# A fused MoE / matrix-LSTM / MoE block on one core: heads normalised without the division, first state copied, squares and sums on ScalarE

## The reference

```python
def step(carry, inp):                       # 8 heads of 64, one token after the other
    c, n, m = carry
    qt, kt, vt, it, ft = inp
    m_t = jnp.maximum(ft + m, it)
    ie = jnp.exp(it - m_t)
    fe = jnp.exp(ft - m_t + m)
    c = fe[:, :, None, None] * c + ie[:, :, None, None] * jnp.einsum('bhd,bhe->bhde', vt, kt)
    n = fe[:, :, None] * n + ie[:, :, None] * kt
    num = jnp.einsum('bhde,bhe->bhd', c, qt)
    den = jnp.maximum(jnp.sum(n * qt, -1, keepdims=True), 1.0)
    return ((c, n, m_t), num / den)
...
h = o * jnp.moveaxis(hs, 0, 1).reshape(Bs, Sl, HID)
hn = _layernorm(h.reshape(Bs, Sl, H, HD), mh_g, mh_b).reshape(Bs, Sl, HID)   # per head, eps 1e-6
out = (hn + x_skip) * jax.nn.silu(r_t)
return out @ W_down.T + b_down + x
```

## Time and profile before

| what | value |
|---|---|
| median of 3 runs | 446.38 us (444.79 to 449.3) |
| the profiled run | 445.47 us |
| its span, first to last instruction | 443.2 us |
| TensorE busy | 384.7 us, 87% |
| VectorE busy | 340.3 us, 77% |
| ScalarE busy | 225.1 us, 51% |
| GpSimd busy | 126.4 us, 29% |
| the three looped sequences and the last | about 127 to 376 us of the span |

### The profile page before, as it was taken

How to read it: one execution, slowest core, us unless ns; L and a number is a source line. 1 busy time by engine, 2 the same in 40 slices (tenths; PEclk the granted TensorE clock), 3 DMA queues, 4 the chain that set the end, 5 groups by cost and what they waited for, 6 DMA issues and landing times.

```text
span 443.2 us, 11327 instructions
## 1 busy us (share of the span) xinstructions
PE 384.7 (87%) x3607; PEld 300.6 (68%) x3629; DVE 340.3 (77%) x1057; ACT 225.1 (51%) x591; POOL 126.4 (29%) x125
## 2 busy tenths in 40 slices
PE   8159999999998899998899898899889957699991
PEld 5023899954776667776668676678667744499991
DVE  4881677767729998969989779999699998567871
ACT  3630444434465565555674555485555651475550
POOL 5574154432003011103110121111021128644552
PEclk9555999999999999999999999999998998989998
DMA  7995122239998787775000000000000522333320
GB/s 208 377 414 187 29 70 71 59 108 214 185 185 185 176 184 177 181 178 124 1 0 0 0 0 0 0 0 0 1 1 1 200 76 83 115 102 93 92 79 1
DMA packets 57264, 46.10 MB, mean 104 GB/s; under 512 B 4111, under 2 KB 53905, under 8 KB 56721
## 3 DMA queue, kind: packets, MB, share of 16 engines
q1 hardware_dynamic: 53618, 37.84, 35.4%
q0 software_dynamic: 2752, 5.73, 3.7%
q10 hardware_dynamic: 864, 2.15, 1.5%
HBM read 17.99 MB, written 27.25 MB: 102 GB/s over the span
## 4 chain that ended last, share of the span: by engine, by line
issue 40%; PE 24%; DVE 11%; POOL 9%; DMA 6%; ACT 4%; SPq 2%; DVEq 1%; POOLq 0%; ACTq 0%
PE bank L896 22%; POOL HS L567 5%; POOL slots L519 3%; DMA K<-consts 2%; DMA XN<-slots 2%; DMA X<-x 1%; ACT WVT L786 1%; PE bank L1033 1%; ACT E L795 1%; POOL LA L561 1%; SPq L418 1%; ACT SELQ L674 1%; DMA QKT<-by_token 1%; DVE W1R L2009 1%; DVE W1R L2011 1%
## 5 line engine op out<-in xcount | busy, mean ns | idle before, releaser
L567 POOL TENSOR_TENSOR HS<-HS,MHALF 128x8 f32<-128x8 f32 x16 | 26.3, 1645 | 145.8 <-DVE HS L2002 145.8
L786 ACT ACTIVATE WVT<-bank,AC 128x128 f32<-128x128 f32 x128 | 36.7, 376 | 28.5 <-PE bank L896 28.5
L896 PE MATMUL bank<-XBT,W1R 128*128 128x128 f32 x368 | 50.4, 281 | 0.3 <-ACT XBT L689 0.3
L896 PE MATMUL bank<-W,HT 128*128 x368 | 49.3, 278 | 0.0
L896 PEld LDWEIGHTS bank<-XBT,W1R 128*128 128x128 f32 x368 | 45.6, 195 | 0.9 <-ACT XBT L689 0.5
L896 PEld LDWEIGHTS bank<-W,HT 128*128 128x128 f32 x368 | 45.4, 194 | 0.4
L696 ACT ACTIVATE HT<-bank,W1R 128x128 f32<-128x128 f32 x115 | 34.8, 365 | 14.9 <-PE bank L896 14.6
L519 POOL DMA_INDIRECT slots<-XN,POS x32 | 32.8, 1025 | 18.2 <-issue 13.0
L896 PE MATMUL bank<-MASKB,IDB 128*128 128x512 bf16 x130 | 34.3, 388 | 3.0 <-POOL HS L567 1.9
L750 ACT ACTIVATE QKT<-bank,COLS 128x512 f32<-128x512 f32 x32 | 22.0, 688 | 26.5 <-PE bank L896 26.5
L1956 DVE TENSOR_TENSOR WOT<-bank,WVT 128x512 f32<-128x512 f32 x32 | 22.0, 686 | 14.5 <-ACT WVT L786 14.4
(11 more groups left out here) (360 smaller groups left out, 987.9 us busy)
## 6 DMA issues: line engine op xcount, KB each, us to landing
slots<-FILL SPq DMA_DIRECT2D x74, 258.0 KB
W<-w SPq DMA_DIRECT2D x2, 2048.0 KB, 15.5
XN<-slots SPq DMA_DIRECT2D x23, 129.0 KB, 2.1
W<-w SPq DMA_DIRECT2D x1, 2064.0 KB, 14.0
slots<-QKT SPq DMA_DIRECT2D x1, 1483.5 KB, 6.1
XB<-slots SPq DMA_DIRECT2D x23, 64.5 KB
X<-x SPq DMA_DIRECT2D x4, 256.0 KB, 5.3
QKT<-by_token SPq DMA_DIRECT2D x4, 256.0 KB, 4.3
```

Of the source, the lines that this page charges most:

```text
L567: g.tensor_tensor(HS[:, 3, :], HS[:, 2, :], MHALF[:, 0:H], ALU.pow).then_inc(roots_ready, 1)
L786: ins = a.activation(DT[:, hf, m, :], DM[:, m * P:(m + 1) * P], ACT.Exp, bias=AC[:, c, h:h + 1])
L896: return t_.matmul(o, l, r, start=start, stop=stop, skip_group_check=True)
```

## The change

The reciprocal and the product with it are left out. The heads stay multiplied by their denominator, and the eps of the layer norm is multiplied by the square of the denominator instead (HEAD_EPS in the clamp, a small product into DN, an addition in `variance`). The gate is multiplied with the numerators straight from PSUM, in two halves. The mean is not subtracted: `centre` gives ScalarE the negative mean, which squares each of the eight heads with it as bias and sums the squares (eight operations in the place of one), and `norm_products` adds it and multiplies by the root in eight operations per chunk. The last chunk of the last sequence keeps the old subtraction and the single Square.

In the first chunk of a sequence the state isn't multiplied and added: ScalarE copies it out of PSUM (`first_state`), VectorE writes only the 65th column. UB is gone. ScalarE scales the rows of the next sequence with the root and a shift (`z_scaled`, in chunk 1), only the first sequence has this on VectorE, in four operations; `add_u` multiplies by one plus the second root and adds a shift.

```diff
--- before.py
+++ after.py
+HEAD_EPS = 1.0e-6
...
-        UB = sb("UB", [P, 4, D])
...
+        z_shift_ready = sem("z_shift_ready")
...
+        cs_copied = sem("cs_copied")
...
+        def last_head(b, c):
+            return isinstance(b, int) and b == NB - 1 and c == NC - 1
...
@@ -712,6 +717,14 @@
                     copy_w1(2, experts[2])
                 over_blocks(act, turn)
 
+            def z_scaled(b):
+
+                act.wait_ge(z_shift_ready, b)
+                for j in range(4):
+                    t = X[:, bass.ds(b * 4 + j, 1), 1:].rearrange("p a d -> p (a d)")
+                    ins = a.activation(ZB[:, j, 1:], t, ACT.Identity, scale=LA[:, 7, j:j + 1], bias=LA[:, 8, j:j + 1])
+                ins.then_inc(z_ready, 1)
+
             def head_in(b):
 
                 act.wait_ge(*pj_full_at(b, "z"))
@@ -795,9 +808,21 @@
                     ins = a.activation(E1[:, m, :], DM[:, m * P:(m + 1) * P], ACT.Exp, bias=MINB[:, c, m:m + 1])
                 ins.then_inc(dm_free, 1)
 
+            def first_state(b):
+
+                act.wait_ge(*tr_read_at(b, "u0"))
+                a.activation(CS[:, :, 0:HD], TR[:, 0:260].rearrange("p (m d) -> p m d", m=4)[:, :, 0:HD], ACT.Copy)\
+                    .then_inc(cs_copied, 1)
+
             def squares(b, c):
                 act.wait_ge(cen_ready, b * NC + c + 1)
-                a.activation(SQ[:, :, :], H2[:, :, :], ACT.Square).then_inc(sq_ready, 1)
+                if last_head(b, c):
+                    a.activation(SQ[:, :, :], H2[:, :, :], ACT.Square).then_inc(sq_ready, 1)
+                    return
+                for h in range(H):
+                    ins = a.activation(SQ[:, h, :], H2[:, h, :], ACT.Square, bias=HS[:, 0, h:h + 1],
+                                       accum_out=HS[:, 1, h:h + 1])
+                ins.then_inc(sq_ready, 1)
 
             def out_t(b, c):
 
@@ -832,9 +857,13 @@
                     take(*nxt, "s")
                 elif last:
                     layer_norm(1, 0)
+                if c == 0:
+                    first_state(b)
                 if last and c == 2:
                     xn_channels(1, 0)
                     xn_channels(1, 1)
+                if c == 1 and not last:
+                    z_scaled(b + 1)
                 if c == 2 and not last:
                     head_in(b + 1)
                     head_silu(b + 1)
@@ -1161,6 +1190,8 @@
             def k_tokens(b, c):
 
                 dst = tr_wait(b, f"k{c}")
+                if c == 2:
+                    pe.wait_ge(cs_copied, b + 1)
                 for m in range(4):
                     ins = t_.transpose(dst[:, m * P:(m + 1) * P], KT[:, m, c * P:(c + 1) * P], ident)
                 ins.then_inc(tr_full, 1)
@@ -1218,6 +1249,8 @@
                 if c == 0:
                     pe.wait_ge(cs_ready, b + 1)
                 else:
+                    if c == 1:
+                        pe.wait_ge(cs_copied, b + 1)
                     pe.wait_ge(*tr_read_at(b, f"u{c - 1}"))
 
                 pe.wait_ge(hv_read, n + 1)
@@ -1839,25 +1872,36 @@
 
                 v.tensor_scalar(LA[:, 5, :], LA[:, 3, :], 1.0 + 1e-6, 1e-11, ALU.mult, ALU.add).then_inc(a_var, 1)
                 v.tensor_scalar(LA[:, 4, :], LA[:, 3, :], 1e-5, None, ALU.add).then_inc(a_var, 1)
-                xs = X[:, bass.ds(b * 4, 4), :]
-                do(v.tensor_tensor(UB[:, :, :], xs, bc(LA[:, 0, :], [P, 4, D]), ALU.subtract))
 
             def scale_norm(b):
 
                 dve.wait_ge(a_rstd, 2 * b + 1)
-                halves = [(0, 2, first_z_ready), (2, 4, z_ready)] if isinstance(b, int) else [(0, 4, z_ready)]
-                for lo, hi, ready in halves:
-                    v.tensor_tensor(ZB[:, lo:hi, 1:], UB[:, lo:hi, 1:], bc(LA[:, 7, lo:hi], [P, hi - lo, D - 1]),
-                                    ALU.mult).then_inc(ready, 1)
+                first = isinstance(b, int)
+                shift = v.scalar_tensor_tensor(out=LA[:, 8, :], in0=LA[:, 0, :], scalar=-1.0, in1=LA[:, 7, :],
+                                               op0=ALU.mult, op1=ALU.mult)
+                if not first:
+                    shift.then_inc(z_shift_ready, 1)
+                    return
+                do(shift)
+                for j in range(4):
+                    did(v.tensor_scalar(ZB[:, j, 1:], X[:, j, 1:], LA[:, 7, j:j + 1], LA[:, 8, j:j + 1],
+                                        ALU.mult, ALU.add))
+                    if j % 2:
+                        step.settle()
+                        v.memset(CREDIT[:, j // 2:j // 2 + 1], 0.0).then_inc((first_z_ready, z_ready)[j // 2], 1)
 
             def add_u(b):
 
 
                 dve.wait_ge(a_rstd, 2 * b + 2)
+                did(v.scalar_tensor_tensor(out=LA[:, 9, :], in0=LA[:, 0, :], scalar=-1.0, in1=LA[:, 6, :],
+                                           op0=ALU.mult, op1=ALU.mult))
+                did(v.tensor_scalar(LA[:, 10, :], LA[:, 6, :], 1.0, None, ALU.add))
+                step.settle()
+                dve.wait_ge(z_ready, b + 1)
                 for j in range(4):
                     t = X[:, bass.ds(b * 4 + j, 1), :].rearrange("p a d -> p (a d)")
-                    did(v.scalar_tensor_tensor(out=t, in0=UB[:, j, :], scalar=LA[:, 6, j:j + 1], in1=t,
-                                               op0=ALU.mult, op1=ALU.add))
+                    did(v.tensor_scalar(t, t, LA[:, 10, j:j + 1], LA[:, 9, j:j + 1], ALU.mult, ALU.add))
                 step.settle()
                 xs = X[:, bass.ds(b * 4, 4), :]
                 do(v.tensor_tensor(xs, xs, row("bdown", D).unsqueeze(1).to_broadcast([P, 4, D]), ALU.add))
@@ -1891,7 +1935,6 @@
 
             def reset_state():
 
-                did(v.memset(CS[:, :, 0:HD], 0.0))
                 v.memset(CS[:, :, HD:HD + 1], 1.0).then_inc(cs_ready, 1)
 
             def gate_scans(b):
@@ -1967,6 +2010,13 @@
                 dve.wait_ge(*tr_full_at(b, f"u{c}"))
                 if c == 0:
                     dve.wait_ge(cs_ready, b + 1)
+                    v.tensor_tensor(CS[:, :, HD], DEC[:, 0, :],
+                                    TR[:, 0:260].rearrange("p (m d) -> p m d", m=4)[:, :, HD],
+                                    ALU.add).then_inc(tr_free, 1)
+                    return
+                if c == 1:
+                    dve.wait_ge(*tr_read_at(b, "u0"))
+                    dve.wait_ge(cs_copied, b + 1)
                 do(v.tensor_tensor(CS[:, :, :], CS[:, :, :], bc(DEC[:, c, :], [P, NP_, HD + 1]), ALU.mult))
                 v.tensor_tensor(CS[:, :, :], CS[:, :, :], TR[:, 0:260].rearrange("p (m d) -> p m d", m=4),
                                 ALU.add).then_inc(tr_free, 1)
@@ -1977,35 +2027,47 @@
                 n = b * NC + c
                 sums = [NB_[hf][:, 0:260].rearrange("p (m d) -> p m d", m=4) for hf in range(2)]
                 h2 = H2[:, :, :].rearrange("p (m two) d -> p two m d", two=2)
+                opened = OT[:, c % 2, :].rearrange("p (m two d) -> p two m d", two=2, d=HD)
                 for hf in range(2):
                     dve.wait_ge(hv_full, 2 * n + hf + 1)
-                    did(v.tensor_scalar(DN[:, 0, hf, :], sums[hf][:, :, HD], 1.0, 2.0, ALU.max, ALU.mult))
+                    did(v.tensor_scalar(DN[:, 0, hf, :], sums[hf][:, :, HD], 1.0, 2.0 * HEAD_EPS ** 0.5,
+                                        ALU.max, ALU.mult))
+                    if hf == 0:
+                        step.settle()
+                        dve.wait_ge(*pj_read_at(b, f"o{c}"))
+                    ins = v.scalar_tensor_tensor(out=h2[:, hf], in0=opened[:, hf], scalar=1.0,
+                                                 in1=sums[hf][:, :, 0:HD], op0=ALU.add, op1=ALU.mult)
+                    if hf == 0:
+                        did(ins)
+                        step.settle()
+                ins.then_inc(hv_read, 1)
+                dve.wait_ge(hv_read, n + 2)
                 step.settle()
-                do(v.reciprocal(DN[:, 1, :, :], DN[:, 0, :, :]))
-                did(v.tensor_tensor(h2[:, 0], sums[0][:, :, 0:HD], bc(DN[:, 1, 0, :], [P, NP_, HD]), ALU.mult))
-                step.settle()
-                v.tensor_tensor(h2[:, 1], sums[1][:, :, 0:HD], bc(DN[:, 1, 1, :], [P, NP_, HD]), ALU.mult)\
-                 .then_inc(hv_read, 1)
-                dve.wait_ge(hv_read, n + 2)
-                dve.wait_ge(*pj_read_at(b, f"o{c}"))
-                flat = H2[:, :, :].rearrange("p h d -> p (h d)")
-                do(v.scalar_tensor_tensor(out=flat, in0=OT[:, c % 2, :], scalar=1.0, in1=flat,
-                                          op0=ALU.add, op1=ALU.mult))
+                did(v.tensor_tensor(DN[:, 1, :, :], DN[:, 0, :, :], DN[:, 0, :, :], ALU.mult))
                 do(v.tensor_reduce(HS[:, 0, :], H2[:, :, :], AX_X, ALU.add))
-                do(v.tensor_scalar(HS[:, 0, :], HS[:, 0, :], 1.0 / HD, None, ALU.mult))
```

(22 more changed lines are left out.)

## The result

| what | before | after |
|---|---|---|
| median on the same chip | 445.59 us (443.95 to 449.3) | 469.9 us (469.57 to 470.31) |
| ratio | 1 | 1.0534 [1.0465, 1.0603] |
| span of the profiled run | 443.2 us | 468.4 us |
| VectorE busy | 340.3 us | 319.4 us |
| ScalarE busy | 225.1 us | 260.9 us |

The changed kernel is 5.3% slower; forecast were 468 us. VectorE did get 21 us less work. Where the 25.2 us of span lie is read from one mark per chunk, the start of the scaled q (VectorE, `scale_q`), in both timelines; the numbers are distances in us.

What follows compares the result with a forecast made beforehand. Not busy time but the chain between engines was taken as bound, with squares ahead of what TensorE waits for. Three passes 17.4, last 4.4, start 0.6: +22.4, span 465.6, plus 2.3 outside, 468 us; range 447 to 480.

Steps and rivals of the forecast that it cites:

- Squares 0.34 apart and 2.8 us: ScalarE, each chunk: eight squares by head with bias and sum take 2.8 us (2.1 to 3.8) instead of 0.63.
- Normalisation 1.9: VectorE, each chunk: eight operations by head take 1.9 us with the wait instead of 0.72, +1.2.
- `centre` 2.2: VectorE, each chunk: without reciprocal, full pass and subtraction, centre takes 2.2 us instead of 3.7, -1.5.
- The sum's own small operation: ScalarE squares: each head's sum brings one more small operation, overlapped, taken at 0.09 us.
- z on ScalarE: ScalarE, once per pass: scaling z adds 1.6 us where it waits for TensorE over 2 us, costing nothing.
- The chain: Attention loop, third pass: delays of +0.7, +2.0 and +4.9 at chunks 1 to 3; the pass +5.8 us longer.
- VectorE's wait in front of `variance` of chunk 0: VectorE, chunk 0: variance waits for the squares from 265.2 to 269.4, so the saved time turns into a wait.
- Three passes 17.4: Unrolled loop: each of three passes is +5.8 us longer, 17.4 in all, read from the third pass's times.
- rival C: TensorE: longer waits lower its granted clock in every pass, +11 us, 479 us; chance 0.18 together with a dearer accumulating sum.
- A: Squares cheap enough to hide, VectorE's 6.2 us per pass count, bounded by TensorE's waits: 432 us; chance 0.12.
- the squares move the pass by 4.5 us for each us: ScalarE's queue, four places per pass: each us of squares lengthens the pass by some 4.5 us.
- B: Floor of both prices, squares 2.1 us and normalisation +0.65: 0.95 us per pass, 450 us; chance 0.20.

Runs made afterwards that it cites:

- e5: The changed kernel with idle TensorE products filling its waits for the copy of o and at r in chunk 3: 466.84 us, ratio to before 1.0481.
- e1: The changed kernel with the old squares, sums and normalisation in every chunk, the rest of the change kept: 433.18 us, ratio to before 0.9781.
- e10: The changed kernel with the old squares, subtraction and normalisation, the same kernel as e1 run once more: 433.45 us, ratio to before 0.9749.
- e3: The changed kernel with eight squares and their bias but without the sum, variance from a constant: 455.13 us, ratio to before 1.0234.
- e9: The changed kernel with eight squares and their sum but without the bias, normalisation still by head: 456.75 us, ratio to before 1.0245.
- e4: The changed kernel with one Square over all heads, without bias and sum, normalisation still by head: 438.01 us, ratio to before 0.9893.
- e6: The changed kernel with squares behind the copies of o and r and the state decays, variance and normalisation moved back too: 473.61 us, ratio 1.0626.

## Why the prediction was right

**The place and the prices.** Squares 0.34 apart and 2.8 us: 0.33 and 2.65. Normalisation 1.9: 1.88. `centre` 2.2: it runs from 275.71 to 278.03, 2.3. The sum's own small operation, taken at 0.09, is that read-out. By the estimate from the Trainium skill (VectorE: DVE Perf Modes, The TRN2 errata) squares and norm step would have been 1.9 and about 1.0 us, and the time near 450; the traces decided for the rows. z on ScalarE (1.65 us) and the first state were hidden, as was said: the decays behind z still waited 0.73 us for TensorE in the third pass.

**The chain.** VectorE's wait in front of `variance` of chunk 0 was put at 265.2 to 269.4, 4.2 us: 4.14. Third pass, measured from the scaled q of chunk 0, which was put at its old place: +0.6 for chunk 1, +1.8 for chunk 2, +4.7 for chunk 3 (predicted +0.7, +2.0, +4.9), XTL +2.6 (2.7), end of the squares of chunk 2 +4.7 (4.9), TensorE's wait for k0 1.17 (1.2), the gated output +5.7 (5.8), its wait at TensorE 0.48 (0.5), the pass 69.0 (69.0). The last sequence's attention part came out +4.2 for 4.4.

**The term that was mis-sized.** "Three passes 17.4" is 21.0. The sum took the third pass for all; the first and second were 8.7 and 6.7. This is rival C, in part: the granted clock fell at two places of the first pass and at one of the second, and e5, which fills the waits, takes 3.9 us out of the three passes and makes them 68.9 to 69.05. The rival's condition, a wait of 2 us for the copy of o, came in every pass, but the clock did not fall in every one; where it fell at both places, the pass was 2.9 us longer than the third, near the rival's 3.2. In all the sum has 22.4 where the span grew by 25.2: 3.6 too little for the passes, 0.2 too much for the last sequence, 2.3 too much for the start, which came out at -1.7 instead of +0.6, and nothing for the end, which is 1.7 longer. Start and end vary by that much for other kernels too, so that the start made up for most of the passes is luck.

**The rivals.** A put the time without the squares' cost at 432 us, 14 less than before, by TensorE's waits. The nearest kernels without that cost, e1 and e10, are 9.6 and 11.5 us faster than before on their chips. So the bound was about right, and its condition was not met. That the squares move the pass by 4.5 us for each us came out at 4.0 to 4.2 for the first 0.7 us (e3, e9) and at 3.2 to 3.5 for all 2.0 (e4), at full clock. B asked for 0.25 per head; even e9, at 0.24 by leaving out the bias, is at 457 and not 450, but it has the normalisation's 1.9 us whole, where B counts its floor.

**What the theory lacked.** Its rule of 4.5 us per pass for each us names one way by which the squares cost time, their place in ScalarE's queue. The sum also carries the later normalisation into the next chunk, but e6 shows how near the second way is: moved behind o and E, the squares cost as much through the chain from the heads to the gated output. From which price of the squares on the second way binds was not measured.

## What to carry to other kernels

Before work is moved from a busy engine to an idle one, look at what it will stand in front of in the new engine's queue: here VectorE got 21 us less to do and waited for ScalarE instead. Cutting one operation of 512 elements into eight, to have an operand per partition and a sum for nothing, multiplied its price by four on ScalarE (0.63 to 2.65 us) and by 2.6 on VectorE (0.72 to 1.88); count the bias and the sum, each of them, before the reductions that they save. And when a step can be reordered out of one wait, add up the length of the loop it is in first: e6 moved it and gained nothing.

## What the hardware showed that I had not expected

- A ScalarE activation with a sum is two instructions. The read-out is 214 ns alone, 0.09 us between starts, and cost as much as the bias did (e3 and e9, 13 us each).
- The same wait of TensorE, 1.95 us for the copy of o, was followed by a granted clock of 0.66 in the first pass, 0.62 in the second and 1.00 in the third. A wait of 1.65 us in the kernel before was followed by 0.51. So the length of a wait does not by itself say what the clock does.
